# The first part's projections: half of the causal convolution by VectorE from a plain product, the other half folded into TensorE's weights

## The reference

```python
x = x + _L0_attn_ref(_layernorm(x), ...)           # the first part
# in it, with D_INNER = 256, D_CONV = 4, D_STATE = 16:
xz = x @ in_proj_w                                 # x: layer norm of the layer norm, with ln1_g, ln1_b
xi, z = jnp.split(xz, 2, axis=-1)
xc = lax.conv_general_dilated(xi.transpose(0, 2, 1), conv_w, window_strides=(1,), padding=[(D_CONV - 1, 0)],
                              feature_group_count=D_INNER, ...)   # each channel: 4 taps over time, causal
xc = _silu(xc + conv_b[None, :, None]).transpose(0, 2, 1)
x_dbl = xc @ x_proj_w
dt, Bm, Cm = jnp.split(x_dbl, [DT_RANK, DT_RANK + D_STATE], axis=-1)
dt = jax.nn.softplus(dt @ dt_proj_w + dt_proj_b)
_, ys = lax.scan(step, h0, xs)                     # the scan over time, from dt, Bm, Cm, xc
y = (ys.transpose(1, 0, 2) + D * xc) * _silu(z)
return y @ out_proj_w                              # then a feed-forward layer
```

## Time and profile before

| | |
|---|---|
| median of 3 runs | 1400.39 us (1397.42 to 1402.18) |
| the profiled execution's own time | 1401.11 us |
| its span, first to last instruction | 1399.4 us |
| PE, DVE, ACT, POOL busy over the span | 1105.9, 892.5, 680.1, 573.1 us |
| mean granted clock of TensorE | 0.909 |

### The profile page before, as it was taken

One profiled execution on the slowest core, in us unless ns is written; L12 is line 12 of the kernel. 1 busy time (PEld: TensorE's weight loads), 2 busy tenths in 40 slices (PEclk: granted clock), 3 DMA queues, 4 the chain that ended last, 5 costly groups with the idle time before them and its releaser, 6 DMA issues. The chain is left out here.

```text
span 1399.4 us, 25149 instructions
## 1 busy us (share of the span) xinstructions
PE 1105.9 (79%) x8340; PEld 714.4 (51%) x8349; DVE 892.5 (64%) x2981; ACT 680.1 (49%) x1256; POOL 573.1 (41%) x739
## 2 busy tenths in 40 slices
PE   8876777679278644299936999859995999899998
PEld 3322222227178633199934777634333777654545
DVE  3599899995545456377549888743858778850200
ACT  2685466545134301132216888627664888641221
POOL 6188889882734414544435434120013655110000
PEclk9989999999589955599968999979996999999999
DMA  2999000000522215311120000020002000000000
GB/s 61 161 191 167 0 0 1 0 0 9 182 61 58 69 38 206 70 42 46 33 72 1 2 3 3 2 57 1 1 0 85 3 3 2 3 1 0 15 0 15
DMA packets 80456, 58.31 MB, mean 42 GB/s; under 512 B 14043, under 2 KB 69221, under 8 KB 80326
## 3 DMA queue, kind: packets, MB, share of 16 engines
q1 hardware_dynamic: 74630, 45.20, 15.3%
q0 software_dynamic: 4544, 9.38, 1.8%
q10 hardware_dynamic: 1152, 2.10, 0.4%
HBM read 28.13 MB, written 28.52 MB: 40 GB/s over the span
## 5 line engine op out<-in xcount | busy, mean ns | idle before, releaser
L713 PE MATMUL bank<-hC,ident 128*128 128x512 f32 x256 | 132.7, 643 | 48.7 <-POOL hC L998 46.7
L998 POOL TENSOR_TENSOR hC<-h,Cs 128x1024 f32<-128x1024 f32 x64 | 150.8, 2356 | 49.8 <-DVE h L897 49.5
L897 DVE TENSOR_TENSOR_SCAN h<-bank,state,dBx 128x512 f32<-128x512 f32 x128 | 157.3, 1270 | 3.7 <-POOL dBx L991 1.7
L1381 POOL DMA_INDIRECT moe_answers<-moe_yw,moe_xg x78 | 84.3, 1081 | 128.6 <-DVE moe_yw L1558 69.7
L2549 DVE CUSTOM_DVE_ANT_0 decay_below<-bank,decay_q_mask 128x256 bf16<-128x256 f32 x256 | 97.2, 419 | 23.0 <-PE bank L2361 22.1
L713 PEld LDWEIGHTS bank<-hC,ident 128*128 128x128 f32 x256 | 46.0, 197 | 111.2 <-POOL hC L998 71.8
L2549 DVE CUSTOM_DVE_ANT_0 window_below<-bank,window_q_mask 128x192 bf16<-128x192 f32 x256 | 80.4, 353 | 29.5 <-PE bank L2361 27.9
L810 ACT ACTIVATE bank<-dt,A 128x512 f32<-128x512 f32 x128 | 83.2, 683 | 28.1 <-DVE h L897 27.1
L1452 PE MATMUL bank<-moe_xgT,moe_wac 128*128 128x128 f32 x624 | 87.4, 286 | 6.5 <-issue 4.1
L2489 ACT ACTIVATE decay_pb<-bank 128x512 f32<-128x512 f32 x128 | 76.2, 598 | 33.3 <-PE bank L2376 32.7
L1467 PE MATMUL bank<-moe_wd,moe_hT 128*128 x624 | 83.0, 277 | 5.7 <-DVE moe_hT L1545 2.7
(11 more groups left out here) (480 smaller groups left out, 2834.2 us busy)
## 6 DMA issues: line engine op xcount, KB each, us to landing
moe_slots<-blank SPq DMA_DIRECT2D x16, 1040.0 KB, 17.6
moe_xg<-moe_slots SPq DMA_DIRECT2D x78, 65.0 KB, 1.9
moe_wa<-in_moe_w SPq DMA_DIRECT2D x2, 2048.0 KB, 9.5
moe_back<-moe_answers SPq DMA_DIRECT2D x8, 256.0 KB, 5.6
moe_back<-moe_answers ACTq DMA_DIRECT2D x8, 256.0 KB, 5.7
moe_wu<-in_moe_wu SPq DMA_DIRECT2D x1, 2048.0 KB
deep_w<-in_deep_w SPq DMA_DIRECT2D x3, 512.0 KB
moe_answers<-moe_yw,moe_xg POOLq DMA_INDIRECT x78, 2.5
```

The source lines that it names most:

```text
L713: last = nc.tensor.matmul(sum_bank(hh)[:], k.ident[:], hC[:, u % 2, hh, :], start=(n == 0), stop=(n == NS - 1))
L897: v.tensor_tensor_scan(h[:, u % 2, hh, :], decay_bank(u, hh)[:], dBx[:, u % 2, hh, :], state[:, n, hh:hh + 1], ALU.mult, ALU.add).then_inc ...
L998: g.tensor_tensor(hC[:, u % 2], h[:, u % 2], Cs[:, u % 2, None, :].to_broadcast([P, H, CW]), ALU.mult).then_inc(q_hC, 1)
L1381: nc.gpsimd.indirect_dma_start(answers, bass.IndirectOffsetOnAxis(index, 0), yw[:, i % NY, :], None)\
```

## The change

The second half of the inner channels is no longer convolved by PE. Before, both halves were computed by four shifted matmuls each. Now PE computes for the second half one plain product xi (`bank[1]`), ACT copies it to SBUF (`take_xi`, into the storage of `k.xnT`), DVE convolves it along the tokens (`convolve`: a multiplication with the last tap, then three multiply-and-add instructions with the input moved by one, two and three tokens, each waiting for the one before), and ACT applies Silu and the bias (`take_conv`). The accumulator lies in the storage of `dBx`. The first half stays as it was. The tap weights of the second half come by a DMA of their own, one column of four taps per partition, in pieces of four bytes.

```diff
-        cwr = sb("cwr", [1, KC * DI])
+        cwr = sb("cwr", [1, KC * P])
+        cw1 = sb("cw1", [P, KC])
...
+        xi = k.xnT
+        conv = dBx[:, :, 0, :]
...
                 for c in range(1, C):
                     x_chunk(c)
+                sp.dma_start(cw1[:], t["conv_wT"][:, P:2 * P].rearrange("k d -> d k")).then_inc(w_cv, 16)
...
+            def convolve(c):
+                acc = conv[:, c % 2, :]
+                wait(dve, s_xc, H * (c - 2) + 2 if c >= 2 else 0)
+                if c == 0:
+                    dve.wait_ge(w_cv, 16)
+                dve.wait_ge(s_xic, c + 1)
+                v.tensor_scalar(acc, xi[:, cols(c)], cw1[:, KC - 1:KC], None, ALU.mult).then_inc(s_cv, 1)
+                for d in range(1, KC):
+                    a = d if c == 0 else 0
+                    dve.wait_ge(s_cv, KC * c + d)
+                    v.scalar_tensor_tensor(out=acc[:, a:CW], in0=xi[:, c * CW + a - d:(c + 1) * CW - d],
+                                           scalar=cw1[:, KC - 1 - d:KC - d], in1=acc[:, a:CW], op0=ALU.mult, op1=ALU.add)\
+                        .then_inc(s_cv, 1)
...
-            for n in range(2):
-                dve.wait_ge(s_cw, n + 1)
-                two = slice(n * KC // 2, (n + 1) * KC // 2)
-                v.tensor_tensor(taps_w[:, two, :], bank[4 + n][:].rearrange("p (k d) -> p k d", d=DI),
-                                inw[:, None, 0:DI].to_broadcast([P, KC // 2, DI]), ALU.mult).then_inc(s_tw, 1)
+            dve.wait_ge(s_cw, 1)
+            v.tensor_tensor(taps_w[:, :, 0:P], bank[4][:].rearrange("p (k d) -> p k d", d=P),
+                            inw[:, None, 0:P].to_broadcast([P, KC, P]), ALU.mult).then_inc(s_tw, 1)
...
             normalise(1)
+            convolve(0)
             dve.wait_ge(w_xp, 16 * 6)
             for c in range(last_c):
                 if c + 2 < C:
                     normalise(c + 2)
+                convolve(c + 1)
...
-                for n in range(2):
-                    nc.tensor.matmul(bank[4 + n][:], k.ones[0:1, :], cwr[:, n * CW:(n + 1) * CW], start=True, stop=True)\
-                        .then_inc(s_cw, 1)
+                nc.tensor.matmul(bank[4][:], k.ones[0:1, :], cwr[:], start=True, stop=True).then_inc(s_cw, 1)
...
             def taps(c):
+                pe.wait_ge(s_tev, c + 1)
+                wait(pe, s_xic, c)
+                nc.tensor.matmul(bank[1][:], inw[:, P:2 * P], xpad[:, PAD + c * CW:PAD + (c + 1) * CW], start=True, stop=True)\
+                    .then_inc(s_xi, 1)
...
+                for j in range(KC):
+                    last = nc.tensor.matmul(bank[0][:], taps_w[:, j, 0:P], xpad[:, c * CW + j:c * CW + j + CW],
+                                            start=(j == 0), stop=(j == KC - 1))
+                last.then_inc(s_in, 1)
...
+            def take_xi(c):
+                act.wait_ge(s_xi, c + 1)
+                nc.scalar.activation(xi[:, cols(c)], bank[1][:], ACT.Copy).then_inc(s_xic, 1)
...
+            def take_conv(c):
+                act.wait_ge(s_cv, KC * (c + 1))
+                nc.scalar.activation(xc[:, 1, cols(c)], conv[:, c % 2, :], ACT.Silu, bias=cb[:, 1:2]).then_inc(s_xc, 1)
...
             for c in range(last_c):
+                take_xi(c + 1)
                 take_taps(c + 1)
                 if c + 2 < C:
                     take_turned(c + 2)
                 take_gate(c + 1)
+                take_conv(c + 1)
```

More of the change, by code:

```diff
@@ L320, in mamba @@
         x_in = [k.sem(f"x_in{c}") for c in range(C)]
-        w_in, w_xp, w_out = k.sem("w_in"), k.sem("w_xp"), k.sem("w_out")
+        w_in, w_xp, w_out, w_cv = k.sem("w_in"), k.sem("w_xp"), k.sem("w_out"), k.sem("w_conv")
         c_zero, c_id, c_more, c_warm = (k.sem("c_" + n) for n in ("zeroed", "ident", "more", "warm"))
@@ L329, in mamba @@
         dt_bank = lambda c, hh: bank[5 + hh] if c < last_c else bank[hh]
+        s_xi, s_xic, s_cv = (k.sem("m_" + n) for n in ("xi", "xi_taken", "conv"))
         s_bc, s_hi, s_lr, s_r1, s_mid, s_r2, s_lo = (k.sem("m_" + n) for n in ("bc", "hi", "lr", "rt1", "mid", "rt2", "lo"))
@@ L389, in project_sync @@
                 x_chunk(0)
-                sp.dma_start(cwr[:], t["conv_wT"].rearrange("(o k) d -> o (k d)", o=1)).then_inc(w_in, 16)
+                sp.dma_start(cwr[:].rearrange("o (k d) -> o k d", k=KC),
+                             t["conv_wT"][:, 0:P].rearrange("(o k) d -> o k d", o=1)).then_inc(w_in, 16)
                 sp.dma_start(inw[:], t["in_proj_w"]).then_inc(w_in, 16)
@@ L567, in taps @@
             def taps(c):
+                pe.wait_ge(s_tev, c + 1)
+                wait(pe, s_xic, c)
+                nc.tensor.matmul(bank[1][:], inw[:, P:2 * P], xpad[:, PAD + c * CW:PAD + (c + 1) * CW], start=True, stop=True)\
+                    .then_inc(s_xi, 1)
                 if c == 0:
[L569 to L576, removed]
+                    pe.wait_ge(s_tw, 1)
+                wait(pe, s_xc, H * (c - 1) + 1 if c else 0)
+                for j in range(KC):
+                    last = nc.tensor.matmul(bank[0][:], taps_w[:, j, 0:P], xpad[:, c * CW + j:c * CW + j + CW],
+                                            start=(j == 0), stop=(j == KC - 1))
+                last.then_inc(s_in, 1)
             def gate(c):
@@ L627, in take_turned @@
                                      scale=g1[:]).then_inc(s_tev, 1)
+            def take_xi(c):
+                act.wait_ge(s_xi, c + 1)
+                nc.scalar.activation(xi[:, cols(c)], bank[1][:], ACT.Copy).then_inc(s_xic, 1)
             def take_taps(c):
[L630 to L633, removed]
+                act.wait_ge(s_in, c + 1)
+                nc.scalar.activation(xc[:, 0, cols(c)], bank[0][:], ACT.Silu, bias=cb[:, 0:1]).then_inc(s_xc, 1)
+            def take_conv(c):
+                act.wait_ge(s_cv, KC * (c + 1))
+                nc.scalar.activation(xc[:, 1, cols(c)], conv[:, c % 2, :], ACT.Silu, bias=cb[:, 1:2]).then_inc(s_xc, 1)
             def take_gate(c):
@@ L654, in project_scalar @@
             take_turned(0)
+            take_xi(0)
             act.wait_ge(w_xp, 16 * 6)
@@ L658, in project_scalar @@
             take_gate(0)
+            take_conv(0)
             for c in range(last_c):
+                take_xi(c + 1)
                 take_taps(c + 1)
```

## The result

The changed kernel takes 1405.56 us (median of 7 runs, 1403.81 to 1408.14), the kernel before on the same chip 1400.69 (7 runs, 1397.42 to 1402.18). The ratio is 1.0034, 95% interval 1.0024 to 1.0044: slower by about a third of a per cent. The prediction's bound of 0.3% lies inside the interval, so whether "same" or "slower" holds by it can't be told. The forecast, 1402.0, was 3.6 us low; the time lies inside the range.

What follows compares the result with a forecast made beforehand. PE was taken to bound the first stage by busy time. Sum: +0.7 (`turn(3)`) - 2.6 (chunk 3's saving) + 3.5 (slow clock) = +1.6 us, forecast 1402.0, range 1396 to 1407.

Steps and rivals of the forecast that it cites:

- PE's saving and the early moves: First stage: twelve chunk matmuls fewer save 10.3 us, one fewer in `spread_taps` 1.5; DVE's early work moves up 1.5 us.
- The convolution's cost: On DVE, per chunk: one TENSOR_SCALAR of 0.43 us and three SCALAR_TENSOR_TENSORs of 0.69 each, 2.5 us undisturbed.
- Chunk 1's convolution beside the selects: DVE alternates with POOL's memset and three `affine_select` over `sel`, so `convolve(1)` takes 14 us instead of 2.5, ending about 36.0.
- What is queued behind it: DVE's rank, rest, outer norm and `normalise(3)` follow `convolve(1)`; PE waits for the last, `turn(3)` at about 41.0 against 40.28.
- the hole: PE's idle time in front of `turn(3)`, from 31 to 41 us, expected at 6 to 10 us; it eats PE's gain.
- PE's clock behind the hole: Idle PE drops to 1.2 GHz; slow work after `turn(3)` costs 3.5 us, bounds nothing to 6.
- the start's price: PE's slow beginning at the kernel's start, where the first eight tap matmuls cost 2.56 us extra.
- ACT's extra eviction and `convolve(3)`: Some 0.7 us a chunk on ACT lies beside PE; `convolve(3)` falls beside `add_bias(1)` but is due later: both cost nothing.
- The DMA of `cw1`: 512 four-byte pieces on SP's queue behind the x chunks, needed by `convolve(0)` at 15.4 us: costed at nothing.
- The whole gain (1): Rival: nothing blocks DVE, the first stage ends 10 to 12 us sooner, time 1390; chance 4%.
- the half one (2): Rival: POOL blocks only DVE's TENSOR_SCALARs, `turn(3)` at about 37.3, gain 3 to 5.6 us, time 1396; chance 12%.
- Rival 3: Slower by the clock: PE stays at 1.2 GHz longer behind the hole; 8 us of loss gives +6.1, 1406.5; chance 14%.

Runs made afterwards that it cites:

- the filler kernel: The changed kernel with 11 matmuls of 512 columns, whose result nobody reads, ahead of `turn(3)`: 1399.39 us, ratio 0.9984 to the kernel before.
- cut selects: The changed kernel with POOL's three `affine_select` over `sel` cut to 16 elements a partition: 1395.37 us, ratio 0.9947 to the kernel before.

## Why the prediction came out as it did

*PE's saving and the early moves*: right. `turn(0)` at 7.52 (forecast 7.4), taps of chunk 2 through at 30.95 (31.0), `convolve(0)` through at 18.3 (18.0).

*The convolution's cost*: right, a little low. TENSOR_SCALAR 0.47 (0.43), three SCALAR_TENSOR_TENSORs 2.33 (2.07).

*Chunk 1's convolution beside the selects*: right, and shown by two experiments. From 22.43 to 35.60 it took 13.2 us (forecast 22.2 to 36.0).

*What is queued behind it*: right. From the convolution's end to `turn(3)` 5.2 us (forecast 5.0 to 5.2); the hole 9.84 (6 to 10), `turn(3)` at 40.78, 41.09, 40.87 and 41.27 in four profiles, mean 41.0 (forecast 41.0). Against the two profiles of before (40.28, 40.46) that is +0.6, where the sum had +0.7.

*PE's clock behind the hole*: right in kind, too small on average, and with too narrow an edge. The first `dBx` came at 71.22, 67.51, 67.9 and 71.6, mean 69.6, against 66.5 in the two profiles of before, so +3.0 where the sum had +1.6. From `turn(3)` to the start of the last row of `steps_dt` the four took 23.97, 19.53, 20.17 and 23.91 us, the filler kernel, whose clock stayed up, 17.68. So the clock cost 6.3, 1.9, 2.5 and 6.2 us, mean 4.2, where the sum had "a little over the start's price, 3.5" and 6 as its edge. I had one row on how soon the clock comes back under dense work, the kernel's start, and gave the value next to it; the rows after 64 us, where the clock was back only after 12 us, had the other. The 8-row matmuls behind the hole, which I named, are where the long executions stay slow: in the short ones the clock was up before them or early in them. Whether they are the reason was not tried.

*ACT's extra eviction and `convolve(3)`*: wrong; a term that was put at nothing. "Lies beside PE" holds for chunks 0 to 2, where no row of PE waits for it, but at the end of the stage ACT's queue is the path. `convolve(3)`, beside `add_bias(1)`, took 3.21 us instead of 2.33, ACT waited for it up to 0.3 us and then took 0.7 us for `take_conv(3)`: from the last row of `steps_dt` to the first `dBx` it is 6.9 us in the two short executions and in the filler kernel, 6.5 in the two long ones, and 5.9 in the kernel before. That is 0.8 on average, and +0.6 - 2.6 + 4.2 + 0.8 is the +3.0 measured.

*The DMA of `cw1`*: right. `convolve(0)` starts at 15.47, straight behind `normalise(1)`, without a wait.

*What the prediction had no term for*: the branch near 930 us. It spoke of the change only through the start of the scan. With the stage's +3.0 on top of 1400.7 the time would be 1403.7, inside "same"; what carried it up to the bound is, as far as the profiles count, the longer wait at the branch. That the time lies in the range although this was missing from the sum is owed to the range's width.

*The rivals.* The whole gain (1) and the half one (2) fell with the row 22.93, 12.67 us. Rival 3, slower by the clock, decided "from a loss of 6.1 us on": two executions of four were just there (6.3 and 6.2), the mean of 4.2 was not, and a loss of 0.3% is reached only together with the branch. So the forecast (70%) had the mechanism, with the sign of its sum; rival 3 (14%) had the size of the loss, for part of its reason.

## What to carry to other kernels

Before moving work to VectorE because its busy share is low, lay its new instructions over GpSimd's timeline: here what read two SBUF tensors, or was a TENSOR_SCALAR of SBUF data, waited out whole GpSimd instructions (12.67 us for 2.33, 7.97 for 1.11), and so did all that was queued behind it. The cure was to move GpSimd's long instructions together with the one step that PE waits for; moving the instructions alone only changed the victim (moving the step alone was not tried). Price a hole of PE twice, as its length and as the slow clock behind it, and take for the second a range from several rows, not the nearest row. Look for the engine whose queue ends the stage as well: an instruction more on it costs up to its full length there (0.55 to 1.0 us here, with its wait). And of the 7 to 10 us by which the stage ended sooner about 4 were missing in the time, so look also for places far behind the change that wait differently.

## What the runs showed of the hardware that I had not expected

The time that the granted clock stayed at its lower level behind a hole of 9.3 to 9.9 us came in two lengths in four executions of one program: it ended 3.8 and 5.2 us behind the start of `turn(3)` (at about 44.9 and 46.0) or 12.9 and 12.8 behind it (at about 53.7 and 54.1). Holes of 3.6 and 4.5 us brought the lower clock too (the gate at 3.40 and 2.96 us instead of 1.88), one of 1.02 us did not. The Trainium skill, "TensorE: Matmul & The Clock Gate", section "Part 1: The HAM clock gate (the "warmup" mystery)", says of the start of a kernel that the number of slow matmuls differs from run to run of the same kernel; behind a hole in its middle these four executions show the same.

The four small TENSOR_SCALARs of `normalise(2)` took 4.25 us beside the memset of `sel`, with full and with cut selects alike, and 7.97 when they reached into the first select as well: one TENSOR_SCALAR was held by a memset and another by a select, while a SCALAR_TENSOR_TENSOR with its accumulator in PSUM went through a select untouched. Which operands a DVE instruction has mattered more than its size.

The wait at the branch near 930 us had two values too, 2.7 to 2.8 and 5.9 to 6.3 us. What decides between them stays open.
